# Scores in two halves of the array, and values' products, projections and outputs in single products between units of scores

## The reference, cut to what matters

```
x = layernorm(x + attention(x)); x = layernorm(x + ffn(x))      # four layers
# attention of layers 0, 2 and 3
q, k, v = x @ Wq.T + bq, x @ Wk.T + bk, x @ Wv.T + bv           # layer 0: rope on q and k
p = softmax(where(key <= query, q @ k.T * scale, -inf))         # 32 heads, 16 channels each
y = (p @ v) @ Wo.T + bo
```

## Time and profile before

| | |
|---|---|
| median of 3 runs | 2105.11 us (2103.57 to 2106.55) |
| profiled execution | 2105.01 us, span 2102.9 us |
| granted TensorE clock, mean | 0.967 of 2.4 GHz |
| busy: PE, DVE, ACT, POOL | 93%, 52%, 37%, 36% of the span |
| unit loops of stages 0, 2, 3 | about 58 to 252, 1452 to 1667, 1780 to 1971 us |

### The profile page before, as it was taken

One profiled execution on the slowest core, in us unless ns is written; L12 is line 12 of the kernel. 1 busy time (PEld: TensorE's weight loads), 2 busy tenths in 40 slices (PEclk: granted clock), 3 DMA queues, 4 the chain that ended last, 5 costly groups with the idle time before them and its releaser, 6 DMA issues.

```text
span 2102.9 us, 28210 instructions
## 1 busy us (share of the span) xinstructions
PE 1962.9 (93%) x10552; PEld 1245.9 (59%) x10552; DVE 1089.8 (52%) x1971; ACT 775.4 (37%) x1647; POOL 747.5 (36%) x1203
## 2 busy tenths in 40 slices
PE   5899967999999999999999899979999997999897
PEld 3454435777777777777776687844444454544443
DVE  4666466555555555555555324135556354566345
ACT  1565523333333333333333233322455402565411
POOL 1455315434343434343432344322344312343300
PEclk9899979999999999999999899999999998999998
DMA  7223000101010101010100234115333006111101
GB/s 196 39 40 104 2 20 1 51 1 51 1 51 1 51 1 51 1 50 1 51 1 30 76 106 170 46 29 64 47 62 102 31 1 77 32 33 46 52 0 40
DMA packets 46200, 95.01 MB, mean 45 GB/s; under 512 B 7689, under 2 KB 35721, under 8 KB 43017
## 3 DMA queue, kind: packets, MB, share of 16 engines
q1 hardware_dynamic: 43474, 90.86, 16.9%
q10 hardware_dynamic: 2592, 2.36, 0.7%
HBM read 62.20 MB, written 2.10 MB: 31 GB/s over the span
## 4 chain that ended last, share of the span: by engine, by line
PE 83%; DVE 7%; ACT 2%; DMA 2%; issue 2%; POOL 1%; ACTq 1%; POOLq 0%; SPq 0%; DVEq 0%
PE PS L1365 11%; PE PS L1434 9%; PE PS L1417 7%; PE PS L1390 7%; PE PS L444 5%; PE PS L547 5%; PE PS L1776 5%; PE PS L525 5%; PE PS L491 5%; PE PS L572 3%; PE PS L1402 3%; PE PS L1376 3%; PE PS L1789 3%; PE PS L1747 2%; PE PS L459 2%
## 5 line engine op out<-in xcount | busy, mean ns | idle before, releaser
L965 ACT ACTIVATE PB<-PS 128x512 f32<-128x512 f32 x480 | 281.5, 600 | 240.6 <-PE PS L525 237.7
L741 DVE TENSOR_REDUCE NM<-PS 128x2 f32<-128x1024 f32 x192 | 209.2, 1091 | 185.7 <-PE PS L493 184.6
L870 POOL TENSOR_SCALAR_AFFINE_SELECT PB<-PB 128x256 f32<-128x256 f32 (+1 forms) x480 | 174.2, 367 | 322.9 <-ACT PB L965 316.9
L1564 ACT COPY PRT<-PS 128x512 f32<-128x512 f32 (+3 forms) x256 | 108.9, 426 | 415.6 <-PE PS L1402 409.8
L491 PE MATMUL PS<-KQ 96*128 96x512 bf16 (+3 forms) x768 | 189.1, 311 | 46.4 <-DMA KQ<-LOW 31.6
L1524 DVE TENSOR_REDUCE NX<-PS 128x1 f32<-128x512 f32 (+3 forms) x256 | 124.3, 490 | 171.2 <-PE PS L1391 169.2
L1677 POOL TENSOR_SCALAR PR<-PR,RCP 128x512 f32<-128x512 f32 (+3 forms) x256 | 135.7, 535 | 201.4 <-DVE RCP L1512 194.8
L525 PE MATMUL PS<-KQ 99*128 99x512 bf16 (+3 forms) x768 | 183.8, 305 | 5.6 <-DMA KQ<-NMT 2.5
L1390 PE MATMUL PS<-kT,qT 128*128 128x512 f32 (+3 forms) x512 | 184.0, 441 | 4.3 <-ACT PR L1622 4.1
L444 PE MATMUL PS<-XTT,WA 128*128 128x512 f32 x288 | 146.8, 617 | 13.5 <-DVE ident_masks_b L2314 12.0
L1622 ACT ACTIVATE PR<-PS,NX 128x512 f32<-128x512 f32 (+3 forms) x256 | 136.5, 533 | 46.9 <-DVE NX L1524 45.7
(11 more groups left out here) (285 smaller groups left out, 3965.7 us busy)
## 6 DMA issues: line engine op xcount, KB each, us to landing
KQ<-HI SPq DMA_DIRECT2D x90, 128.0 KB, 4.0
KQ<-MID SPq DMA_DIRECT2D x72, 128.0 KB, 4.7
WB<-f_w SPq DMA_DIRECT2D x12, 768.0 KB, 4.4
WB<-w1o SPq DMA_DIRECT2D x8, 1024.0 KB, 7.9
WC<-f_w SPq DMA_DIRECT2D x10, 768.0 KB, 4.4
WB<-w1a SPq DMA_DIRECT2D x8, 768.0 KB, 4.4
WB<-w1b SPq DMA_DIRECT2D x8, 768.0 KB, 5.9
WA<-w SPq DMA_DIRECT2D x6, 1024.0 KB, 6.4
```

What stands on the lines that cost most here:

```text
L741: x = dve.tensor_reduce(nm[:, h:h + 2, i], PS[:, b:b + 2, 0:(i + 1) * P], AX.X, ALU.max, negate=True)
L870: pool.affine_select(blocks, blocks, [[0, count], [1, P]], ALU.is_ge, 0.0, base=0, channel_multiplier=-1).then_inc(s16["probs_ready"].sem, 1)
L965: act.activation(PB[:, n % PBS, :], PS[:, 4 + n % 2, :], ACT.Exp, scale=self.scale)\
```

## The change

What is computed stays the same; how q, k and the maxima are split and where products stand changes.

- q and k are split into two fp32r parts (KQ is F32R): `high` rounds, `take` writes the low part itself; REST, `middle` and POOL's `low` are gone. Three products of parts matter, so a head needs 3 x 16 = 48 rows, and 50 with the maxima's two.
- Of each two heads one lies in rows 0 to 49, the other in rows 64 to 113 (`par`). Every score product names its half with `tile_position=(64 * par, 0)`. In the loop each product of `scoresT` is followed by one of `scores` of the same width for the other half. The first pass has 5 units of maxima (UNITS) instead of 6; masks are added by `masks`, on 64 rows each, at odd k.
- Each chunk's rows come by six DMAs again (`row`: three rows for each half), the maxima's by two. Loads of late chunks stand at other units (`load_at`), and the slots of KQ rotate by three pairs of units.
- `aside` now comes last in its slot. Projections stand at k = 5 to 8, one product each, the second sequence's values at k = 4, 5, 8, 9 (stage 2) or 5 to 8, the outputs at k = 6 to 9.
- `max_T` writes to bank 6 and waits for `self.aux`. VectorE's `take`, `turn` and the tail's `mean` of the unit before move ahead of the unit's maxima (`ahead`).
- The constant of ones for KQ comes from SBUF, and SP waits for it before its first load.

```diff
-SR = 6 * HD
-MR = 3
+SR = 3 * HD
+MR = 2
...
-PASS1 = ((3, 0, 2), (0, 0, 4), (3, 2, 4), (2, 0, 2), (2, 2, 4), (1, 0, 4))
+UNITS = (((3, 0, 0),), ((3, 1, 0),), ((2, 0, 0), (0, 0, 384)), ((2, 1, 0), (0, 1, 384)), ((1, 0, 0), (1, 1, 256)))
+NUNIT = len(UNITS)
...
-        KQ = sb("KQ", [P, 48, T], BF16, A16)
+        KQ = sb("KQ", [P, 28, T], F32R, A16)
...
-            def query(self, G, h):
-                return (G // 2 % 3 if self.wide else G // 2 % NC) * 8 + G % 2 * 4 + h
-            def key(self, G, h):
-                return 24 + self.query(G, h) if self.wide else 32 + G
+            def query(self, G, j):
+                return G // 2 % 3 * 4 + G % 2 * 2 + j
+            def key(self, G, j):
+                return 12 + (self.query(G, j) if self.wide else G)
...
+            def scores(self, pe, G, a, par, x):
+                on, u = self.on, NUNIT * G + a
+                if par and x == 0:
+                    if u >= 2:
+                        pe.wait_ge(on["max_ready"].sem, on["max_ready"].at(u - 1))
...
+                i, j, at = UNITS[a][x]
+                n, rows = (i + 1) * P, slice(64 * par, 64 * par + SR)
+                pe.matmul(PS[:, 2 * (u % 2) + par, at:at + n], KQ[rows, self.query(G, j), i * P:(i + 1) * P],
+                          KQ[rows, self.key(G, j), 0:n], start=(x == 0), stop=False, tile_position=(64 * par, 0))
+            def masks(self, pe, G, a):
+                u = NUNIT * G + a
+                for x, (i, j, at) in enumerate(UNITS[a]):
+                    for half in range(2):
+                        for par in (1, 0):
+                            rows, far = slice(64 * par, 64 * par + 64), 2 * (half != par)
+                            to = slice(at + i * P + 64 * half, at + (i + 1) * P)
+                            ins = pe.matmul(PS[:, 2 * (u % 2) + par, to], ident_masks_b[rows, far, :],
+                                            ident_masks_b[rows, far + 1, 64 * half:P], start=False,
+                                            stop=(half == 1 and x == len(UNITS[a]) - 1), tile_position=(64 * par, 0))
+                ins.then_inc(s16["scores_ready"].sem, 1)
+            def unit(self, pe, G, a):
+                for x in range(len(UNITS[a])):
+                    for par in (1, 0):
+                        self.scores(pe, G, a, par, x)
+                self.masks(pe, G, a)
             def max_T(self, pe, G):
                 on = self.on
                 pe.wait_ge(on["max_parts"].sem, on["max_parts"].at(G + 1))
-                pe.transpose(PS[0:MR * 16, 3, 0:P // 2].bitcast(BF16), NM3[:, G % 2, :], identb[:, :])\
+                pe.wait_ge(*self.aux)
+                pe.transpose(PS[0:MR * 16, AUX, 0:P], NM2[:, G % 2, :].bitcast(F32), ident[:, :])\
                   .then_inc(s16["maxT_psum"].sem, 1)
+            def blocks(self, k):
+                if k < 4:
+                    return ((k, 0, 0),)
+                if k < 8:
+                    return (k - 4, 1, 0), (k - 4, 3, 384)
+                return (k - 8, 2, 0), (k - 6, 2, 256)
...
+            def scoresT(self, pe, s, k, x):
...
+                h, j, at = self.blocks(k)[x]
+                par, rows = h % 2, slice(64 * (h % 2), 64 * (h % 2) + SR + MR)
+                ins = pe.matmul(PS[:, 4 + n % 2, at:at + T - j * P], KQ[rows, self.key(s, h // 2), j * P:(j + 1) * P],
+                                KQ[rows, self.query(s, h // 2), j * P:T], start=(x == 0),
+                                stop=(x == len(self.blocks(k)) - 1), tile_position=(64 * par, 0))
+                if x == len(self.blocks(k)) - 1:
+                    ins.then_inc(s16["scoresT_ready"].sem, 1)
...
-                if self.wide and s == 0:
-                    if k < 4:
-                        self.project(pe, 6, k)
-                    elif 5 <= k < 9:
-                        self.project(pe, 7, k - 5)
-                first = 1 if self.wide else 6
-                if s in self.late and first <= k < first + NC:
-                    self.project(pe, self.late[s], k - first)
-                if self.wide and s in (1, 2) and 1 <= k <= 8:
-                    self.project_v(pe, 1, 2 * s - 2 + (k - 1) // 4, (k - 1) % 4)
-                if not self.wide and s == 3 and k >= 6:
+                t = s - self.out_step
+                if self.wide and s == 0 and k in (5, 8):
                     for c in range(NC):
-                        self.project_v(pe, 1, k - 6, c)
-                t = s - self.out_step
+                        self.project(pe, 6 if k == 5 else 7, c)
+                if s in self.late and 5 <= k <= 8:
+                    self.project(pe, self.late[s], k - 5)
+                if self.wide and s in (1, 2) and k in (4, 5, 8, 9):
+                    for c in range(2):
+                        self.project_v(pe, 1, 2 * s - 2 + (k >= 8), c + 2 * (k in (5, 9)))
+                if not self.wide and s == 3 and 5 <= k <= 8:
+                    for c in range(NC):
+                        self.project_v(pe, 1, k - 5, c)
                 if 0 <= t - 2 < NT and k == 5:
                     self.turn_first(pe, t - 2)
-                if 0 <= t < NT and k >= 7:
-                    for c in ((0,), (1,), (2, 3))[k - 7]:
-                        if c == 0:
-                            pe.wait_ge(*self.aux)
-                        x = self.out_part(pe, 0, t, c, AUX)
+                if 0 <= t < NT and 6 <= k:
+                    if k == 6:
+                        pe.wait_ge(*self.aux)
+                    x = self.out_part(pe, 0, t, k - 6, AUX)
...
-                        self.scoresT(pe, s, k)
-                        self.aside(pe, s, k)
-                        if more and k in (0, 1, 2, 5, 6, 7):
-                            self.scores(pe, s + 2, (0, 1, 2, 5, 6, 7).index(k))
+                        for x in range(len(self.blocks(k))):
+                            self.scoresT(pe, s, k, x)
+                            if more:
+                                self.scores(pe, s + 2, k // 2, 1 - k % 2, x)
+                        if more and k % 2:
+                            self.masks(pe, s + 2, k // 2)
                         if k == 1 and s >= 3 and s % 2:
                             self.ctx_T(pe, (s - 3) // 2, 7)
-                        if k == 3 and s + 1 < last:
-                            self.max_T(pe, s + 1)
+                        if k == 3:
+                            if s + 1 < last:
+                                self.max_T(pe, s + 1)
                         if 3 <= k <= 5 and s:
                             self.pv(pe, s - 1, k - 3)
                         if k == 8 and s:
                             self.back(pe, s - 1)
+                        self.aside(pe, s, k)
...
+            def ahead(self, dve, st, s):
+                t = s - self.out_step
+                if s - 1 in self.late:
+                    self.turn(dve, self.late[s - 1]) if self.rope else self.take(dve, self.late[s - 1])
+                if self.wide and s in (2, 3):
+                    self.take_v(dve, 1, 2 * s - 3)
+                if not self.wide and s == 4:
+                    self.take_v(dve, 1, 0)
+                if 0 <= t - 1 < NT:
+                    self.tails[0].mean(dve, st, t - 1, PS[:, AUX, :])
             def beside(self, dve, st, s, a):
                 t = s - self.out_step
-                if self.rope and a == 1 and s - 2 in self.late:
-                    self.take(dve, self.late[s - 2])
...
-                if a == 2 and not self.wide and s - 1 in self.late:
-                    self.turn(dve, self.late[s - 1]) if self.rope else self.take(dve, self.late[s - 1])
...
-                if a == 2 and 0 <= t - 2 < NT:
-                    self.tails[0].finish(dve, t - 2)
-                if a == 2 and 0 <= t - 1 < NT:
-                    self.tails[0].mean(dve, st, t - 1, PS[:, AUX, :])
-                if a == 5 and self.wide and s in self.late:
-                    self.take(dve, self.late[s])
+                if self.rope and a == 2 and s - 1 in self.late:
+                    self.take(dve, self.late[s - 1])
+                if a == 1 and 0 <= t - 1 < NT:
+                    self.tails[0].finish(dve, t - 1)
...
+                for par in range(2):
+                    sp.dma_start(KQ[64 * par + SR:64 * par + SR + MR, a:a + 2, :].bitcast(F32),
+                                 NMT[16 * par:16 * par + 16, G % 2, :].bitcast(F32))\
+                      .then_inc(s16["max%d_loaded" % (G % 2)].sem, 16)
+            def row(self, eng, m, r, part):
+                b, kind, i = self.chunks[m]
+                a, n = (self.query(2 * NC * b + 2 * i, 0), 4) if kind == "q" else \
+                    (self.key(2 * NC * b + 2 * i, 0), 4 if self.wide else 8)
+                for par in range(2):
+                    to = slice(64 * par + r * HD, 64 * par + (r + 1) * HD)
+                    eng.dma_start(KQ[to, a:a + n, :].bitcast(F32), (part[par::2, :] if n == 4 else part).bitcast(F32))\
```

(15 more changed lines are left out.)

370 lines of the change are left out of this document (135 added, 235 removed).

## The result

The changed kernel takes 2186.72 us (median of 4 runs, 2184.14 to 2189.17) against 2105.07, a ratio of 1.039 with a 95% interval of 1.037 to 1.041. Slower, as forecast, but by 82 us, not by 30, and just outside the range. The profiled execution spans 2187.5 us, 84.6 more than before. TensorE is busy 20 us longer, at a mean clock of 0.946 of 2.4 GHz (0.967 before); VectorE, ScalarE and POOL are busy less, as the edits say.

What follows compares the result with a forecast made beforehand. TensorE's own sum was taken to bind, with some 0.8 us of waits a unit. Terms 11.5 + 7.7 + 5.5 + 15 - 6 gave +34, taken as +30 on 2105: 2135 us, range 2070 to 2185.

Steps and rivals of the forecast that it cites:

- Beginnings: Ways to the stages' first scores: removed steps save 2 us a stage, -6 in all, between -15 and +10.
- Rival (d): DMA: beginnings lose 5 us in stages 0 and 3 instead of gaining, 2150 us; counted within the forecast's chance of 0.43.
- TensorE's sum: TensorE's own work per unit: plain from 8.9 to 8.05 us, loaded (with a projection) from 12.3 to 12.45.
- Entries: TensorE switching tile shape drains: 0.20 us each with 128-column fp32 weights; +1.1 a plain unit, +2.1 a loaded one.
- pairs: Transposed and maximum products in opposite row halves run together: 2.6 us a unit instead of 4.4, 1.8 saved.
- (b): The two halves' weights load one after the other: 0.8 us more in each of 42 units, 2169 us; chance 0.14.
- (c): The two halves don't stream together: 1.4 us more in each of 42 units, 2194 us; chance 0.08.
- The turn's 5.5 us: Stage 0, VectorE's turn delays max_T: +1.5 in units 5, 7 and 9, +0.5 in 2 and 3.
- Loops: Unit loops of three stages: loaded units +11.5 us, outputs +7.7, stage 0's turns +5.5, last units +15, plain units nothing.
- Rival (a): Faster: entries fall into TensorE's waits for ScalarE or VectorE; 2091 us if half hides, 2045 if all; chance 0.35.
- Outputs: Units with output products at k=6 to 9: +0.7 us each, 11 units, +7.7.
- Last two units: Each stage's last two units, without maxima to pair: fp32r +0.4, entries 2.1, so +2.5 us each, 6 units, +15.

Runs made afterwards that it cites:

- e1_held: Changed kernel, but in stages 0 and 3 SP holds the third chunk's rows back until those of the first two have landed: 2173.2 us.
- e12_keys: e11_five, but in stages 0 and 3 the first chunk's odd key heads load behind the first two chunks, with the fill there cut to match: 2129.8 us.
- e11_five: Kernel with the four edits, plus products nobody reads ahead of TensorE's wait for the first rows of each stage: 2135.6 us.
- e5_half: Changed kernel, but in the unit loops both products of a pair lie in the same half of the array: 2328.3 us.
- e3_norm: Changed kernel, but VectorE norms the previous unit's values ahead of the unit's last maximum, not behind it: 2174.5 us.
- e4_grouped: Changed kernel, but the four products of a late projection stand together at the sixth slot, not one each at slots six to nine: 2190.2 us.
- e8_before_waits: Kernel before, but in each unit's first two slots TensorE waits for the exponential of the transposed scores it has just given: 2198.4 us.
- the four edits: Changed kernel with third chunk's rows held back, norm before last maximum, maxima's transpose behind second values' products, ScalarE's rotated-chunk rounding at fourth slot: 2141.7 us.

## Why the prediction was wrong

**Beginnings: the step that failed.** I took -6 for the three, between -15 and +10; the ways to the loops grew by 38.8, 45 off, most of the miss of 52. The step had the bytes right (2.3 MB for the first two chunks instead of 1.5) and their 4 us, but took these back on the condition that larger packets go faster, which they don't (118 GB/s as before), and kept only the 2 us of the steps that went. What it left out is the chunks behind them: SP issues their rows while ScalarE's queue still holds the first two chunks', the DMA engines serve both, and by the first scores 3.7 MB have been moved. I counted the bytes that the scores need, not those that are in the queues by then. The two parts are shown apart: in stage 0 the first scores come 16.4 us later after their first rows than before; holding the third chunk back takes 9.1 of it away (e1_held), loading half of the keys later 6.9 (e12_keys against e11_five). In stage 3 it is 7.3 and 5.4 of 16.8. Rival (d) had the place right, at +5 a stage, 13 too small for each of stages 0 and 3.

**TensorE's sum: right.** In the chain of the loaded unit 8 of stage 3 TensorE works 12.34 us in a row, where I had 12.45. Entries cost 0.19 to 0.20, and pairs stream together. Rivals (b) and (c) fall with the pairs' starts 3 to 4 ns apart and steps of 0.24 (512 columns), 0.12 (256) and 0.06 (128, where I had 0.11), without an entry. e5_half is rival (c) made real: 1.2 to 1.8 us a unit, where I had 1.4, and the clock on top, where I had nothing. The turn's 5.5 us came out by luck, by another split, and don't hold what its units lost: the plain unit 5 of stage 0, at full clock, lasts 12.19 us instead of 9.68, where I had +1.5.

**Loops: +40 forecast, +44 measured, out of other terms.** A plain unit of stage 3 is as long as before (10.06 against 10.09), as I had it, but by luck too: 0.85 of it is the wait for the norm that I hadn't priced, without which it lasts 9.26. The loaded one was put at 13.65 = 12.45 + 1.2 of waits; it lasts 12.81 in stage 3, with 0.2 of waits. The mistake is to add waits for ScalarE to a unit whose entries already fill them: in stage 3 loaded units even gained 0.2, where I had +0.5; in stage 2 they lost 0.3 to 0.5. Rival (a) was right to that extent. Outputs: +0.1 a unit in stages 0 and 3 and +0.5 in stage 2, not +0.7. Last two units: 3.3 in stage 3 (12.19 + 10.28 against 9.97 + 9.21), 3.2 in stage 0 and 4.2 in stage 2, not 5.

**What I didn't price.** (1) VectorE's norm stands behind the last maximum, which moved from k=7 to k=9; I let TensorE wait 0.2 for the maximum and not 0.85 for the norm that follows it, in 12 units, 10.2 us in all (e3_norm). (2) ScalarE rounds the rotated chunk one unit earlier, and stands for VectorE and POOL with exponentials behind it: 12.9 us. I followed the moved steps of VectorE, not what ScalarE's moved step is queued ahead of. (3) The granted clock, named and left out. Unit 7 of stage 3 lasts 11.58 us with 3.4 at half clock, and 10.07 without any in e4_grouped, which leaves this unit as it is: 0.44 us for each us. The loops have 56 us more of it, by that an estimated 25 us of their 44. Why it falls there is open in part: waits do it (e8_before_waits), and single products of one half of the array seem to (e5_half). After the four edits, which leave the projections' and the transposes' entries in place, the loops are 8.9 us longer than before, nearly all in stage 2: so about 35 of the 44 were order and the clock that follows it, and not, as I had it, entries.

That the total of the loops came out near the forecast proves nothing for its terms.

## What to carry to other kernels

Ahead of a stage's first product count every byte issued by then, on all queues, not only those that it waits for; and hold later transfers back (9.1 and 7.3 us here). When a step is moved in an engine's list, look for what it waits for and what is queued behind it there, and expect two such waits to cover each other: undoing one shows nothing. Work that fills waits is free until it is no longer in them, so a sum of work and waits counts it twice.

## What the hardware showed beyond that

In the changed kernel the granted clock falls to half inside loops in which TensorE is busy 92 to 95% of the time, 3 to 6 us into a unit, mostly behind waits of 0.85 to 2.1 us; once (unit 4 of stage 0) behind waits of 0.19 and 0.38 alone. Such waits don't always do it: units 5, 7 and 9 of stage 3 have the same ones, and it falls in units 7 and 9 only. With the products of a pair in one half of the array (e5_half, its longest execution) it stays low through nearly all of units 0 to 10 of stage 0, at 97% busy, and at the same place in stages 2 and 3 mostly not. Ahead of the first scores packets of 1.6 to 1.7 KB on the mean moved at the same 118 GB/s as packets of 0.9 KB before, at a DMA share of 0.93 to 0.95 instead of 1.13 to 1.14.
